# Expert scales spread by a broadcast read of a DRAM scratch in place of matrix products, and a new order on every engine

## The reference

```python
x = x + conv(_ln_c(x))            # q, k, v products; linear attention, a causal cumulative sum over 2304 tokens, 8 heads
t = _to_tokens(x)                 # [8, 2304, 128]
t = t + ffn(_ln_t(t))
# ffn, for each token:
logits = xf @ gate_w + router_gamma
probs = softmax(logits)
rw, sel = top_k(probs, 2)                         # 2 of 8 experts
combine = sum(one_hot(sel, 8) * rw[..., None])    # [tokens, 8], six zeros a token
eo = einsum('nl,eld->end', xf, expert_w) + expert_b
out = einsum('ne,end->nd', combine, gam * eo + bet)
```

## Time and profile before

| what | value |
|---|---|
| median of 3 runs | 734.6 us (732.08 to 739.66) |
| the profiled execution | 737.64 us, span of its instructions 735.9 us |
| mean granted TensorE clock | 0.978 of 2.4 GHz |
| busy over the span | PE 681.8, DVE 632.3, POOL 468.7, PEld 458.9, ACT 292.0 us |
| DMA | 30.53 MB, mean 41 GB/s |

### The profile page before, as it was taken

How to read it: one execution, slowest core, us unless ns; L and a number is a source line. 1 busy time by engine, 2 the same in 40 slices (tenths; PEclk the granted TensorE clock), 3 DMA queues, 4 the chain that set the end, 5 groups by cost and what they waited for, 6 DMA issues and landing times.

```text
span 735.9 us, 35372 instructions
## 1 busy us (share of the span) xinstructions
PE 681.8 (93%) x13757; PEld 458.9 (62%) x13865; DVE 632.3 (86%) x1690; ACT 292.0 (40%) x865; POOL 468.7 (64%) x696
## 2 busy tenths in 40 slices
PE   3667999989999999999999999999999999999986
PEld 1656656656666666666666666666666666665542
DVE  3667999988999999999999999999999999988762
ACT  1134434433444444444444444444444444434311
POOL 5365765565667676767676767676767676764521
PEclk9788999999999999999999999999999999999997
DMA  4111111111111111111111111111111111011000
GB/s 109 53 35 32 45 32 46 46 45 32 45 43 43 43 43 43 43 43 43 43 43 42 44 42 43 42 44 42 44 42 43 42 43 41 29 31 33 17 17 29
DMA packets 60229, 30.53 MB, mean 41 GB/s; under 512 B 2160, under 2 KB 60176, under 8 KB 60176
## 3 DMA queue, kind: packets, MB, share of 16 engines
q1 hardware_dynamic: 60176, 29.79, 14.2%
HBM read 20.34 MB, written 9.44 MB: 40 GB/s over the span
## 4 chain that ended last, share of the span: by engine, by line
PE 82%; issue 8%; POOL 4%; DVE 4%; DMA 1%; ACT 1%; SPq 0%; DVEq 0%; POOLq 0%; ACTq 0%
PE bank_o L1134 31%; PE num L1048 7%; PE num L1031 5%; PE wide_a L1128 4%; PE wide_a L1000 3%; PE num L1015 3%; PE bank_g L1071 3%; PE bank_g L960 3%; PE bank_g L911 3%; PE bank_g L1086 2%; PE bank_g L975 2%; PE wide_a L943 2%; PE bank_o L1093 2%; PE wide_a L945 2%; PE wide_b L943 2%
## 5 line engine op out<-in xcount | busy, mean ns | idle before, releaser
L1134 PE MATMUL bank_o<-xs,e_w 128*128 128x512 f32 x576 | 279.7, 610 | 0.2 <-DVE xs L774 0.2
L1134 PEld LDWEIGHTS bank_o<-xs,e_w 128*128 128x128 f32 x576 | 99.3, 191 | 88.0 <-issue 87.5
L338 POOL TENSOR_TENSOR qn<-feat,rden 128x512 f32<-128x512 f32 x36 | 38.8, 1077 | 114.0 <-DVE rden L654 114.0
L374 POOL TENSOR_TENSOR xs<-spread,x 128x1024 f32<-128x1024 f32 x36 | 97.7, 2714 | 4.4 <-ACT spread L498 4.4
L774 DVE TENSOR_TENSOR xs<-wide_a,x 128x1024 f32<-128x1024 f32 x72 | 87.5, 1215 | 6.2 <-PE wide_b L1128 6.1
L456 ACT ACTIVATE q_eo<-bank_g,parity 128x512 f32<-128x512 f32 x72 | 45.5, 683 | 96.3 <-PE bank_g L975 96.3
L465 ACT ACTIVATE squares<-bank_g 128x128 f32<-128x128 f32 x108 | 28.5, 274 | 137.3 <-issue 70.0
L326 POOL TENSOR_TENSOR k_sum<-k_sum,feat 128x64 f32<-128x64 f32 x216 | 68.8, 318 | 16.9
L637 DVE SCALAR_TENSOR_TENSOR feat<-ex,qkv 128x512 f32<-128x512 f32 x72 | 79.3, 1103 | 0.0
L366 POOL TENSOR_TENSOR coef<-weight,coef 128x256 fp32r<-128x256 f32 x36 | 26.1, 724 | 83.0 <-ACT coef L486 83.0
L307 POOL TENSOR_TENSOR x_low<-x,x_high 128x512 fp32r<-128x512 f32 x36 | 61.1, 1697 | 4.6 <-ACT x_high L421 4.6
(11 more groups left out here) (161 smaller groups left out, 1630.7 us busy)
## 6 DMA issues: line engine op xcount, KB each, us to landing
x<-in_x SPq DMA_DIRECT2D x36, 256.0 KB, 2.9
x_res<-in_x SPq DMA_DIRECT2D x36, 256.0 KB, 2.9
out<-o SPq DMA_DIRECT2D x36, 256.0 KB, 2.5
beta_raw<-in_L_ffn_beta_w SPq DMA_DIRECT2D x1, 512.0 KB
e_raw<-in_L_ffn_expert_w SPq DMA_DIRECT2D x1, 512.0 KB
w_raw<-in_L_conv_Wkv SPq DMA_DIRECT2D x2, 64.0 KB, 2.4
b_qkv<-in_L_conv_bkv SPq DMA_DIRECT2D x1, 128.0 KB, 6.1
w_raw<-in_L_conv_Wq SPq DMA_DIRECT2D x1, 64.0 KB, 2.5
```

The lines of the kernel that those rows point to most:

```text
L374: tt(xs[:, g.par, 2 * pair:2 * pair + 2], spread[:], flat(x1[:, g.par]).unsqueeze(1) .broadcast_to([128, 2, U * T]), ALU.mult).then_inc(S[ ...
L1134: last = mm(bank_o[:], e_w[:, e], xs[:, g.par, e], start=False, stop=(final and e % 2 == 1), skip_group_check=True)
```

## The change

The router's weights are no longer spread by PE. `coef` holds the coefficients, `pack` holds for each image four blocks of eight columns (scale, high part, low part, high part again), and one PE transpose turns all of it, where four were needed. ACT copies the transposed block twice: to `scale_t` (plain, for the scratch) and in four small pieces to `coef_t` (for `bias`). SP then writes the scales of the four images to a DRAM scratch `scale_d` by four DMAs, waits until they have landed, and reads the scratch back with one DMA that gives all 128 partitions the same 16 KB (8 experts x 512 tokens, 2.1 MB in all) and lands in `xs`. DVE and POOL multiply `x1` into `xs` in place, DVE three pairs and POOL one, as before. The three loads of a blank weight tile, which stood ahead of products on PE, are now increments of an unused semaphore. The order of the calls in every engine's `step` is new, and `scale_pair` on DVE has age 6 for all of its pairs.

```diff
+        coef = sb("coef", [128, U, EXPERTS])
+        pack = sb("pack", [128, U, 4, EXPERTS])
+        scale_t = sb("scale_t", [128, PAR, T])
...
+        scale_d = [nc.dram_tensor(f"scale_d{b}", (EXPERTS, U, T), F32, kind="Internal").ap() for b in range(PAR)]
...
+            def write_scales(g):
+                need(sp, "scale_evac", g.i + 1)
+                for u in range(U):
+                    sp.dma_start(scale_d[g.par][:, u], scale_t[ROWS * u:ROWS * u + EXPERTS, g.par])\
+                        .then_inc(written[g.par], 16)
+
+            def spread_scales(g):
+                need(sp, "out_done", g.i - 1)
+                sp.sem_inc(S["sp_turn"], 1)
+                sp.wait_ge(written[g.par], 16 * U * (g.half + 1))
+                sp.dma_start(xs[:, g.par], scale_d[g.par].rearrange("e u t -> e (u t)").partition_broadcast(128))\
+                    .then_inc(spread[g.par], 16)
...
-            def scale_pair(g, pair, evac, done):
-                need(pool, evac, g.i + 1)
+                tt(pack[:, :, 2], coef[:], pack[:, :, 1], ALU.subtract).then_inc(S["coef_low"], 1)
+
+            def scale_pair(g, pair):
+                pool.wait_ge(spread[g.par], 16 * (g.half + 1))
                 need(pool, "x1_done", g.i + 1)
-                need(pool, "out_done", g.i - 1)
-                tt(xs[:, g.par, 2 * pair:2 * pair + 2], spread[:], flat(x1[:, g.par]).unsqueeze(1)
-                   .broadcast_to([128, 2, U * T]), ALU.mult).then_inc(S[done], 1)
+                pick = xs[:, g.par, 2 * pair:2 * pair + 2]
+                tt(pick, pick, flat(x1[:, g.par]).unsqueeze(1).broadcast_to([128, 2, U * T]), ALU.mult)\
+                    .then_inc(S[f"scaled{pair}"], 1)
...
-            def spread_pair(g, bank, scaled, done):
-                need(act, "spread1", g.i + 1)
-                need(act, scaled, g.i)
-                nc.scalar.activation(spread[:].rearrange("p n t -> p (n t)"), bank[:], copy).then_inc(S[done], 1)
...
-            def scale_pair(g, pair, spread_done, done):
-                need(dve, spread_done, g.i + 1)
+            def scale_pair(g, pair):
+                dve.wait_ge(spread[g.par], 16 * (g.half + 1))
                 need(dve, "x1_done", g.i + 1)
-                need(dve, "out_done", g.i - 1)
-                tt(xs[:, g.par, 2 * pair:2 * pair + 2],
-                   (wide_a, wide_b)[pair % 2][:].rearrange("p (n t) -> p n t", n=2),
-                   flat(x1[:, g.par]).unsqueeze(1).broadcast_to([128, 2, U * T]), ALU.mult).then_inc(S[done], 1)
+                pick = xs[:, g.par, 2 * pair:2 * pair + 2]
+                tt(pick, pick, flat(x1[:, g.par]).unsqueeze(1).broadcast_to([128, 2, U * T]), ALU.mult)\
+                    .then_inc(S[f"scaled{pair}"], 1)
...
-                nc.tensor.ldweights(blank[:], tile_position=(0, 0))
+                pe.sem_inc(S["turn"], 1)
...
-                for u in range(U):
-                    last = transpose(bank_g[:, T * u:T * u + T],
-                                     coef4[:, u].rearrange("p r s e -> p (r s e)").bitcast(F32), ident[:])
-                last.then_inc(S["ct_done"], 1)
+                transpose(bank_g[:, 0:T], pack[:].rearrange("p u k e -> p (u k e)"), ident[:])\
+                    .then_inc(S["ct_done"], 1)
...
-                for r in range(4):
-                    rows = slice(ROWS * r, ROWS * r + ROWS)
-                    last = mm(w_bank[r], sel[rows, k], coef_t[rows, g.par], start=True, stop=True)
-                last.then_inc(S[done], 1)
```

More of the change, by code:

```diff
@@ L166, in program @@
         r_loaded = [sem(f"r_loaded{b}") for b in range(PAR)]
+        written = [sem(f"written{b}") for b in range(PAR)]
+        spread = [sem(f"spread{b}") for b in range(PAR)]
         stored = [sem(f"stored{b}") for b in range(PAR)]
@@ L244, in step @@
                     load_later(g)
-                g = at(7)
+                g = at(5)
+                if g:
+                    load_residual(g)
+                g = at(6)
+                if g:
+                    write_scales(g)
+                g = at(8)
                 if g:
                     store(g)
-                g = at(3)
+                g = at(6)
                 if g:
-                    load_residual(g)
-            steps(sp, step, 7)
+                    spread_scales(g)
+            steps(sp, step, 8)
             for b in range(PAR):
@@ L288, in _ @@
             made(nc.gpsimd.memset(state[:], 0.0))
-            done = 6
-            for k in range(2):
-                for r in range(4):
[L292 to L301, removed]
+            done = 5
+            for u in range(U):
+                for n, part in ((0, 1), (0, 2), (1, 3)):
+                    select(place[:, n], 128, ROWS * u + EXPERTS * part).then_inc(S["setup"], 1)
+                    done += 1
+                    pool.wait_ge(S["setup"], done)
+            for b in range(PAR):
+                made(nc.gpsimd.memset(coef_t[:, b].bitcast(F32), 0.0))
             pool.wait_ge(S["consts"], CONSTS)
@@ L784, in step @@
             def step(at):
[L785 removed]
+                g = at(5)
                 if g:
[L787 to L790 removed]
+                    attention(g)
                 g = at(4)
                 if g:
+                    denominators(g)
+                    denominators_eps(g)
+                    inverse_denominators(g)
                     key_values(g)
[L794 to L796 removed]
                 g = at(1)
@@ L825, in step @@
                     coefficients(g)
-                    scales(g)
+                g = at(2)
+                if g:
+                    project(g, 3)
+                g = at(5)
+                if g:
+                    scales(g)
+                g = at(6)
+                if g:
+                    scale_pair(g, 1)
+                    scale_pair(g, 2)
+                g = at(4)
+                if g:
+                    causal(g, 1)
+                    causal(g, 0)
+                g = at(2)
+                if g:
+                    features(g, 0)
+                g = at(6)
+                if g:
+                    residual(g)
                 g = at(0)
@@ L1151, in step @@
                     q_transposed(g)
+                g = at(2)
+                if g:
+                    project(g, 3)
                 g = at(6)
                 if g:
-                    experts(g, 0, "scaled0", False)
-                g = at(3)
+                    bias(g)
+                g = at(4)
                 if g:
-                    key_values(g)
+                    from_state(g)
+                g = at(6)
+                if g:
+                    experts(g, 0, False)
+                    experts(g, 3, False)
+                g = at(5)
+                if g:
+                    coef_transposed(g)
+                g = at(4)
+                if g:
+                    scores(g)
+                g = at(6)
+                if g:
+                    experts(g, 1, False)
+                    experts(g, 2, True)
                 g = at(0)
@@ L1178, in step @@
                     k_transposed(g)
-                g = at(4)
+                g = at(1)
                 if g:
-                    values(g)
-                g = at(5)
-                if g:
-                    bias(g)
-                    spread_scales(g, 0, "spread0")
-                    experts(g, 2, "scaled2", False)
-                g = at(4)
-                if g:
-                    x1_centred(g)
+                    project(g, 1)
             first_weights()
```

290 lines of the change are left out of this document (105 added, 185 removed).

## The result

The changed kernel takes **893.95 us** (median of 4 runs, 887.78 to 895.99), the kernel before 735.25 in the same comparison. The ratio is 1.215, with an interval of 1.210 to 1.221. The forecast was 879. The profiled execution took 895.99 with a span of 894.0.

A forecast was written before the change was run, and what follows sets the result against it. PE bounded the old kernel, DVE right behind. New step: DVE 17.28 + collision 3.6 + meetings 0.7 + clock and DMA 0.9 = 22.5; 62.9 + 35 x 22.5 + 30 = 880.4, adjusted to 879 us; range 745 to 1000.

The forecast's parts named there:

- The frame: Whole span: lead of 62.9 before the first router, 35 steps of 22.5, tail of 30, 1.7 outside the span.
- DVE's own work: DVE's work in a loop step without waits, 17.28 us, with in-place products kept at 1.21 each.
- POOL's product and `x_low` against the router: DVE's router links wait for POOL's two SBUF instructions: 3.6 more in each step, bounds 0 and 3.6.
- The other meetings: DVE's other two products and both `features` meet POOL's sums of keys and `qk`: 0.7 a step, 0 to 2.
- The clock and the DMA: PE's clock halving after its wait at the transpose, plus up to 1.4 of unhidden read: 0.9 a step, 0 to 2.2.
- The slow broadcast: Rival: the read of the scratch runs below the queue's 285 GB/s; 1162 us at half rate, 1010 at 200 GB/s; 16%.
- only part of it collides: Rival: POOL and DVE collide partly at the router, 1 to 2.5 a step, 732 to 809 us; 10%.
- POOL's product could run where DVE reads PSUM: Rival: POOL's product and `x_low` avoid the collision, DVE bounds at 17.3 a step, 697 us; 12%.
- PE: PE's work in a step falls from 18.31 to about 16.9, without `spread_scales` and three of four transposes.

The follow-up runs named there:

- run 8: Changed kernel plus three products with a zero tile in PE's wait ahead of the transpose, in the loop's steps alone; 850.80 us, ratio 1.158.
- run 2: Changed kernel with POOL multiplying only 4 of the 512 tokens of its expert pair; 766.63 us, ratio 1.040.
- run 10: Changed kernel with `x_low` behind `rstd1`, SP's `x` load behind the broadcast read, two zero-tile products on PE, all four expert pairs on DVE; 818.28 us.
- run 5: Changed kernel with POOL's `x_low` moved behind `rstd1` and SP's load of `x` moved behind the broadcast read; 856.67 us, ratio 1.166.
- run 7: Changed kernel with POOL's product moved behind the router and DVE's masks ahead of its second and third product; 957.84 us, ratio 1.305.
- run 4: Changed kernel with the broadcast read cut to the scales of two experts, 0.5 MB in place of 2.1 MB; 878.25 us, ratio 1.192.
- run 1: Changed kernel with POOL's `x_low` moved behind `rstd1`, ahead of `qn`, SP's order unchanged; 1058.46 us, ratio 1.439.
- run 6: Changed kernel with POOL's product moved behind the low part of the coefficients and `next_state`, to meet DVE's later in-place products; 852.62 us, ratio 1.160.
- run 11: run 10 without the two zero-tile products on PE; 813.17 us, ratio 1.107.

## Why the prediction was right

*The frame.* Lead 62.1 (forecast 62.9), 35 steps of 22.82 on average (22.5), tail 33.2 (30), 2.0 outside the span (1.7): 896.0 for the profiled execution, where the sum gave 882. Eleven of the 14 us are the steps, 3 the tail. That the lead fits so well is luck in part: in the profiles of the runs it lies anywhere from 56.1 to 69.3.

*DVE's own work*, forecast 17.28. In the step of run 8 DVE stands idle for no other engine, and 21.43 less the waits below is 17.0. This is a remainder, but two other runs leave the same: run 2's step is 19.27 - 0.93 - 1.3 = 17.0, and run 10's is 20.35 - 1.1 for the fourth product - 0.95 - 1.3 = 17.0. The forecast passed over a wait of 0.18 ahead of `qkv` in the step that it read, which makes 17.1 of its 17.28; and the 0.44 that it put down to PE has `issue` in its row. The in-place product takes 1.21 by itself, the value taken.

*POOL's product and `x_low` against the router*, forecast 3.6: 2.15 in `lg0` and 0.93 in `lg`, **3.1** measured. The mechanism is as told; run 2 took out the one wait, run 5 the other, run 10 both, and run 7 put POOL's product beside PSUM readers at no cost to either. It came out 0.5 smaller because the 0.19 that each of the two links needs by itself lies inside its wait, and because `lg` is issued when `x_low` has run for 0.2.

*The other meetings*, forecast 0.7 (0 to 2): in run 8 `feat` 1.47 (+0.8), the second and third product 2.65 together in place of 2.35 (+0.3), `scales` 0.43 (+0.2): 1.3.

*The clock and the DMA*, forecast 0.9 (0 to 2.2): 1.4, which run 8 gives back when the clock stays at 1.00. The DMA's part is zero in the loop (run 4). I had the landing at 14.0 behind the router's end; it was 426.0 - 415.4 = 10.6. The read went out at 3.2 behind it, not 5.2: transpose and copy took less (the first write is issued 1.0 behind it, not 1.6), and the small writes land sooner than the bound from an `x` load. The read then took 7.4 in all, without the 1.4 that I had put around it.

17.0 + 3.1 + 1.3 + 1.4 = 22.8, the measured step. The sum closes by construction, as 17.0 is a remainder and 1.4 a difference; what bears it out are the runs that took its terms out one by one. So no step failed. DVE's own work was taken 0.3 and the collision 0.5 too high, the small meetings 0.6 and the clock 0.5 too low; that these nearly cancel, so that the step is hit to 0.3, is luck.

*The rivals.* The slow broadcast did not come about: 2.1 MB in 7.4 is 283 GB/s, the rate of the queue before, from one 16 KB source. That the two agree says little, for the 7.4 holds a part that does not go with the size: run 4's 0.5 MB took 4.0, so the further 1.6 MB took 3.4. That only part of it collides did not come about either: 3.1 a step were lost, more than its 1 to 2.5. That POOL's product could run where DVE reads PSUM is not what happens in the changed order, but run 7 made it so, and 697 did not follow, because PE's waits took the place. *PE*, forecast 16.9 a step: 17.2 in run 2.

*What stays open.* PE's products, scores and transpose could be ordered anew for run 7's placement; that was not tried. And the runs split the time by cost, not by edit: the order alone, with the scales still spread by PE, was not run.

## What to carry to other kernels

When an operand moves from PSUM to SBUF, list the instructions on the neighbouring engine that run beside it: DVE with two SBUF inputs and POOL take turns, and the price falls on whatever short instruction stands next in the chain, here a 0.2 us link that waited 2.3. A wait moved out of one place must be followed to the next meeting (`x_low` from `lg` to `feat`), through every in-order queue that hangs on it (SP in run 1), and to the engine that wants the result (PE in run 7). Where PE waits in each step, count the clock as well: here it cost 1.4 of 4.4.

## What the runs showed of the hardware that was not expected

- Short POOL instructions pay too: a subtraction of 0.25 took 1.10 and a sum of 0.45 took 1.43 behind DVE's in-place products (run 6). It is so in the changed kernel too, where the sum for `rstd1` at 421.02 took 0.65 in place of 0.20 behind a feature product.
- Not every POOL instruction holds DVE up: `rstd2`'s power runs from 405.92 to 406.94, and DVE's product, which starts in it at 406.43, takes its usual 1.22. The Trainium skill (SBUF — State Buffer, Who interferes with whom) says that DVE and POOL share a pair of ports, which is held for the whole instruction by whoever starts first. The products and `x_low` agree, to 0.1 us; this instruction, which reads 4 elements a partition, does not (the same in all 32 cases of the trace; why is not shown).
- DMA and engines: in the changed kernel `residual` (0.69), the statistics (0.88) and the second feature product (0.67) run beside the read of 2.1 MB. In run 4 the read of 0.5 MB has landed, or all but landed, when they start, and they take the same. The Trainium skill (SBUF — State Buffer, Who interferes with whom) says that DMA never contends with a compute engine, and these rows agree. `lg0` and the in-place products do not run beside the read.
- The clock: stretches at 0.50 from 212 to 720 number 22 in the changed kernel, where PE waits 3.35 a step at the transpose, 16 with waits of 2.45 (run 5), 11 with 1.4 (run 11), three with 0.9 to 1.15 (run 6) and none with 1.2 (run 2), so the length of this wait does not settle it alone.
